# Inverse roots in seven dependent operations, and the first and last token groups gathered, added and stored in halves

## What is computed

```
def _layernorm(x, axis=-1, eps=1e-05):
    m = jnp.mean(x, axis=axis, keepdims=True)
    v = jnp.var(x, axis=axis, keepdims=True)
    return (x - m) / jnp.sqrt(v + eps)
...
x = x + jnp.tanh(g_xattn[0]) * _L0_xattn_ref(_layernorm(x, axis=-1), ctx_1024, ...)
x = x + jnp.tanh(g_ffn[0]) * _L0_ffn_ref(_layernorm(x, axis=-1), ...)
...
x = x + jnp.tanh(g_ffn[3]) * _L3_ffn_ref(_layernorm(x, axis=-1), ...)
```

```
sel = jnp.take_along_axis(expert_out, topk_idx[:, :, None], axis=1)
out = (sel * topk_scores.astype(flat.dtype)[:, :, None]).sum(axis=1)
out = out + jax.nn.silu(flat @ sgate_w.T) * (flat @ sup_w.T) @ sdown_w.T
```

## Time and profile before

| | us |
|---|---|
| median of 3 runs | 1399.87 |
| lowest and highest run | 1396.83, 1408.49 |
| the profiled execution | 1391.09 |
| its span, first to last instruction | 1389.3 |
| TensorE busy | 1218.6 |
| VectorE busy | 717.1 |
| mean granted TensorE clock | 0.916 |

### The profile page before, as it was taken

One profiled execution on the slowest core, in us unless ns is written; L12 is line 12 of the kernel. 1 busy time (PEld: TensorE's weight loads), 2 busy tenths in 40 slices (PEclk: granted clock), 3 DMA queues, 4 the chain that ended last, 5 costly groups with the idle time before them and its releaser, 6 DMA issues.

```text
span 1389.3 us, 19389 instructions
## 1 busy us (share of the span) xinstructions
PE 1218.6 (88%) x6360; PEld 765.9 (55%) x6361; DVE 717.1 (52%) x2061; ACT 448.6 (32%) x842; POOL 293.5 (21%) x347
## 2 busy tenths in 40 slices
PE   5999999999978899989988759999756799999993
PEld 3534434434443445444443649999655555888862
DVE  7263465376985466555752531111176752455556
ACT  3322122223353454454444103333233201333320
POOL 2111111040121111011000041111122564255660
PEclk9999999999988999999998669999976789999997
DMA  9999999110000000000100845555309322455538
GB/s 301 337 338 334 333 335 319 33 31 0 0 1 1 1 0 1 1 1 1 34 1 1 253 146 187 186 184 173 121 15 349 127 91 92 129 167 160 170 112 309
DMA packets 140424, 186.75 MB, mean 134 GB/s; under 512 B 8672, under 2 KB 124896, under 8 KB 140224
## 3 DMA queue, kind: packets, MB, share of 16 engines
q1 hardware_dynamic: 130800, 159.28, 37.0%
q0 software_dynamic: 9552, 26.52, 5.2%
HBM read 83.71 MB, written 102.06 MB: 134 GB/s over the span
## 4 chain that ended last, share of the span: by engine, by line
PE 74%; DVE 13%; ACT 4%; issue 3%; DMA 3%; POOL 2%; SPq 0%; POOLq 0%; DVEq 0%; ACTq 0%
PE psum L1979 14%; PE psum L1258 6%; PE psum L1269 6%; PE psum L1049 6%; PE psum L2191 5%; PE psum L1068 2%; PE psum L930 2%; PE psum L2248 2%; PE psum L2225 2%; PE psum L2272 2%; PE psum L1972 2%; PE psum L2007 2%; DVE arena L2810 2%; PE psum L2169 2%; PE psum L941 2%
## 5 line engine op out<-in xcount | busy, mean ns | idle before, releaser
L1979 PE MATMUL psum<-arena 128*128 128x512 f32 x432 | 205.1, 625 | 0.0
L2810 DVE TENSOR_REDUCE arena<-psum 128x4 f32<-128x616 f32 x128 | 101.6, 797 | 93.7 <-PE psum L2191 92.2
L1979 PEld LDWEIGHTS psum<-arena 128*128 128x128 f32 x432 | 82.9, 199 | 119.7 <-issue 118.9
L2191 PE MATMUL psum<-arena 32*128 32x308 f32 x512 | 103.5, 496 | 18.0 <-DVE arena L2810 16.8
L1176 POOL DMA_INDIRECT ys<-xnT,arena x96 | 92.4, 962 | 93.7 <-DVE xnT L1153 71.1
L2392 ACT ACTIVATE arena<-psum,arena 128x512 f32<-128x512 f32 x72 | 49.0, 685 | 174.3 <-PE psum L1979 164.6
L1870 POOL TENSOR_TENSOR x_tok<-x_tok,add_row 128x1024 f32<-128x1024 f32 x16 | 38.3, 2400 | 275.7 <-ACT xn L1735 275.6
L2483 ACT ACTIVATE arena<-psum 128x2048 f32<-128x2048 f32 x40 | 75.0, 1874 | 59.5 <-PE psum L2229 42.5
L1049 PE MATMUL psum<-arena,xn 128*128 x384 | 87.1, 380 | 2.3 <-ACT xn L1099 1.9
L1258 PEld LDWEIGHTS psum<-side,arena 128*128 128x128 f32 x736 | 87.4, 195 | 2.7 <-ACT side L1303 1.6
L1258 PE MATMUL psum<-side,arena 128*128 128x128 f32 x736 | 87.8, 278 | 1.0 <-ACT side L1303 1.0
(11 more groups left out here) (408 smaller groups left out, 2105.8 us busy)
## 6 DMA issues: line engine op xcount, KB each, us to landing
xs<-zeros SPq DMA_DIRECT2D x8, 8576.0 KB, 59.4
arena<-in_W SPq DMA_DIRECT2D x31, 1024.0 KB, 5.0
xn<-xs SPq DMA_DIRECT2D x64, 134.0 KB, 2.3
arena<-in_gate_up SPq DMA_DIRECT2D x4, 2048.0 KB, 15.7
arena<-ys SPq DMA_DIRECT2D x4, 2048.0 KB, 14.6
arena<-xs SPq DMA_DIRECT2D x32, 134.0 KB, 2.3
arena<-in_down SPq DMA_DIRECT2D x4, 1024.0 KB, 14.5
xs<-zeros SPq DMA_DIRECT2D x1, 2990.0 KB, 18.1
```

The source lines that it names most:

```text
L1979: ins = pe.matmul(bank[dict(hn=4, r=5, z=6, xn=7)[k]][:], lhs[:, cols], r, start=(start and n == 0), stop=(stop and n == len(w) - 1))
L2191: ins = pe.matmul(bank[most_bank(n, k) + i][:, 0:2 * M].rearrange("p (h m) -> p h m", h=2), qhT[rows, n % 3, c, t * P:(t + 1) * P], keys[r ...
L2810: dve.tensor_reduce(neg[:, n % 2, t, 2 * pair:2 * pair + 2, 2 * c:2 * c + 2], psum[:, most_bank(n, k):most_bank(n, k) + 2, 0:2 * M].rearra ...
```

## The change

The nine root steps become seven: one round of the old kind, with factors scaled by `CUBE_GAIN`, and one round of four operations of higher order (y*y; times v; plus a constant, times itself; plus a constant, times y). The start value stays. The list `endings` cuts the token tiles into six pieces: 0-1, 2-3, 4-7, 8-11, 12-13, 14-15. The gathers, the additions in `combine7_vector` and the stores go by these pieces, each with a semaphore of its own and its own count in `x_done`. On DVE the first three pieces (groups 0 and 1) stand before the shared expert's add for the last group, the other three behind it. The title given with the change also speaks of a moved context product; the diff has no edit of one.

```diff
-NEWTON = 3
+CUBE_GAIN = 0.375 ** 0.2
+RSQRT_STEPS = 7
...
+        first_gathered, last_gathered = sem("first_gathered"), sem("last_gathered")
+        endings = [(0, GT // 2, (first_gathered, 16))]
+        endings += [(g * GT + (GT // 2 if g == 0 else 0), (g + 1) * GT - (GT // 2 if g == G - 1 else 0), gathered_in[g].at(7, 16))
+                    for g in range(G)]
+        endings += [(T - GT // 2, T, (last_gathered, 16))]
...
-        xn_ready = Alternate(series("xn_ready_even", {s: G for s in (0, 2, 4, 6)}), series("xn_ready_odd", {s: G for s in (1, 3, 5, 7)}))
+        xn_ready = Alternate(series("xn_ready_even", {s: G for s in (0, 2, 4, 6)}), series("xn_ready_odd", {1: G, 3: G, 5: G, 7: G + 2}))
...
-            for g in range(G):
-                sp.dma_start(gathered7[:, g * GT:(g + 1) * GT],
-                             ys7[1 + g * GN * K4:1 + (g + 1) * GN * K4].rearrange("(t p k) d -> p t k d", p=P, k=K4)
-                             ).then_inc(gathered_in[g].sem, 16)
+            for t0, t1, landed in endings:
+                sp.dma_start(gathered7[:, t0:t1],
+                             ys7[1 + t0 * P * K4:1 + t1 * P * K4].rearrange("(t p k) d -> p t k d", p=P, k=K4)
+                             ).then_inc(landed[0], 16)
...
-        def combine7_vector(dve, ch, g):
-
-            dve.wait_ge(shared_added, 2 * (g + 1))
-            dve.wait_ge(*gathered_in[g].at(7, 16))
-            ch.settle()
-            xs = x_tok[:, g * GT:(g + 1) * GT]
+        def combine7_vector(dve, ch, n):
+
+            t0, t1, landed = endings[n]
+            dve.wait_ge(shared_added, 2 * (t0 // GT + 1))
+            dve.wait_ge(*landed)
+            ch.settle()
+            xs = x_tok[:, t0:t1]
             for k in range(K4):
-                ins = dve.tensor_tensor(xs, xs, gathered7[:, g * GT:(g + 1) * GT, k], ALU.add)
+                ins = dve.tensor_tensor(xs, xs, gathered7[:, t0:t1, k], ALU.add)
...
             combine7_vector(dve, ch, 0)
             combine7_vector(dve, ch, 1)
+            combine7_vector(dve, ch, 2)
             shared_add_vector(dve, G - 1)
-            combine7_vector(dve, ch, 2)
-            combine7_vector(dve, ch, 3)
+            for n in range(3, len(endings)):
+                combine7_vector(dve, ch, n)
...
-            for _ in range(NEWTON):
-                ch.settle(k)
-                ch.step(dve.tensor_tensor(t, y, y, ALU.mult))
-                k = ch.n
-                yield
-                ch.settle(k)
-                ch.step(dve.scalar_tensor_tensor(t, t, -0.5, v, ALU.mult, ALU.mult))
-                k = ch.n
-                yield
-                ch.settle(k)
-                ch.step(dve.scalar_tensor_tensor(y, t, 1.5, y, ALU.add, ALU.mult))
-                k = ch.n
-                yield
+            c = CUBE_GAIN
+            ch.settle(k)
+            ch.step(dve.tensor_tensor(t, y, y, ALU.mult))
...
+            ch.step(dve.scalar_tensor_tensor(t, t, -0.5 * c, v, ALU.mult, ALU.mult))
...
+            ch.step(dve.scalar_tensor_tensor(y, t, 1.5 * c, y, ALU.add, ALU.mult))
...
+            ch.step(dve.tensor_tensor(t, y, y, ALU.mult))
...
+            ch.step(dve.tensor_tensor(t, t, v, ALU.mult))
...
+            ch.step(dve.scalar_tensor_tensor(t, t, -1.25 / c ** 3, t, ALU.add, ALU.mult))
...
+            ch.step(dve.scalar_tensor_tensor(y, t, 1.875 / c, y, ALU.add, ALU.mult))
...
-        SLOT_STEPS = 2 + 3 * NEWTON + 2 * 2 + 2 * 1 + 2 * 1 + 8 * 3
+        SLOT_STEPS = 2 + RSQRT_STEPS + 2 * 2 + 2 * 1 + 2 * 1 + 8 * 3
...
-            for g in range(G):
-                sp.wait_ge(*x_done.at(last_stage, g + 1))
-                sp.dma_start(out.rearrange("(t p) d -> p t d", p=P)[:, g * GT:(g + 1) * GT],
-                             x_tok[:, g * GT:(g + 1) * GT]).then_inc(out_stored, 16)
-            sp.wait_ge(out_stored, G * 16)
+            for n, (t0, t1, _) in enumerate(endings):
+                sp.wait_ge(*x_done.at(7, n + 1))
+                sp.dma_start(out.rearrange("(t p) d -> p t d", p=P)[:, t0:t1], x_tok[:, t0:t1]).then_inc(out_stored, 16)
+            sp.wait_ge(out_stored, len(endings) * 16)
```

More of the change, by code:

```diff
@@ L1656, in rsqrt_newton @@
             k = ch.n
-            for _ in range(NEWTON):
-                ch.settle(k)
-                ch.step(dve.tensor_tensor(t, y, y, ALU.mult))
-                k = ch.n
-                yield
-                ch.settle(k)
-                ch.step(dve.scalar_tensor_tensor(t, t, -0.5, v, ALU.mult, ALU.mult))
-                k = ch.n
-                yield
-                ch.settle(k)
-                ch.step(dve.scalar_tensor_tensor(y, t, 1.5, y, ALU.add, ALU.mult))
-                k = ch.n
-                yield
+            c = CUBE_GAIN
+            ch.settle(k)
+            ch.step(dve.tensor_tensor(t, y, y, ALU.mult))
+            k = ch.n
+            yield
+            ch.settle(k)
+            ch.step(dve.scalar_tensor_tensor(t, t, -0.5 * c, v, ALU.mult, ALU.mult))
+            k = ch.n
+            yield
+            ch.settle(k)
+            ch.step(dve.scalar_tensor_tensor(y, t, 1.5 * c, y, ALU.add, ALU.mult))
+            k = ch.n
+            yield
+            ch.settle(k)
+            ch.step(dve.tensor_tensor(t, y, y, ALU.mult))
+            k = ch.n
+            yield
+            ch.settle(k)
+            ch.step(dve.tensor_tensor(t, t, v, ALU.mult))
+            k = ch.n
+            yield
+            ch.settle(k)
+            ch.step(dve.scalar_tensor_tensor(t, t, -1.25 / c ** 3, t, ALU.add, ALU.mult))
+            k = ch.n
+            yield
+            ch.settle(k)
+            ch.step(dve.scalar_tensor_tensor(y, t, 1.875 / c, y, ALU.add, ALU.mult))
+            k = ch.n
+            yield
             ch.settle(k)
```

## The result

The changed kernel took 1383.03 us in the median of 6 runs (1373.22 to 1386.56), the kernel before in runs on the same chip 1398.35 (6 runs, 1392.30 to 1408.49). The ratio is 0.9896, with a 95% interval from 0.9857 to 0.9935. Forecast were 1393.6 us, a range from 1385 to 1402, and a change within 1%.

What follows compares the result with a forecast made beforehand. The prediction took TensorE as three quarters of the chain, VectorE 13%. Root savings of 1.4 + 0 + 2.5 + 2.7 = 6.6 us and 0.3 lost in the ending gave -6.3: median 1399.87 to 1393.6 us, range 1385 to 1402.

Steps and rivals of the forecast that it cites:

- Start: First 20 us: two 308-wide steps, 1.02 us, plus two pairs of interleaved norm steps, 0.39, together 1.41 us less.
- Slot iterations: Three 128x16 roots lie hidden beside score products: 0 us gained, some 1.2 us at most without that cover.
- Attention stages: Stages with heads, 400 to 770 us: fewer norm steps on the chain, 2.5 us less, bounds 0 and 6.2.
- 58 x 2/9 x 0.196: Attention stages with heads: 58 root steps on the chain, two of nine go, 0.196 us each, 2.5 us saved.
- The upper bound of 6.2: Attention stages with heads: 16 norms saving 0.39 us each, 6.2 us at most.
- C: Rival: slower by TensorE's clock, 2.1 us per block falling to low; three eat the gain, five make 1404; chance 0.12.
- Rival D: Three blocks rising to high clock, 6.3 us, or attention stages 3.7 more: 1387 to 1390, both 1384; chance 0.11.
- a word against C: Argument that less waiting of TensorE should, if anything, leave the clock higher; no size given.
- The text's own sign of being wrong: Profile after: ending over 1 us shorter, slot iterations shorter, or stage lengths differing because the clock does.
- Last context attention: 1004 to 1105 us: seven norms fully on the chain, 0.39 us each, 2.7 us less, bounds 2 and 3.
- Ending: Output put together in six pieces: 0.73 us lost on VectorE, 0.4 gained by the smaller last store, 0.3 us slower.
- The wait for group 1: In the ending, VectorE waits some 1.8 us for group 1's gather; the shared add that could fill it stands behind.

Runs made afterwards that it cites:

- e12: Kernel before with seven root steps only in the three roots of the slot iterations, old ending: 1392.84 us, ratio 0.9993.
- e11: Changed kernel with a six-step root and the last group's shared add ahead of group 1's additions: 1390.09 us, ratio 0.9832.
- e3: Kernel before with only the ending in six pieces, the root in nine steps: 1393.61 us, ratio 1.0006.
- e6: Kernel before with seven root steps everywhere except the layer norms of stages 1 to 5, old ending: 1386.23 us, ratio 0.9944.
- e1: Kernel before, unchanged, run again against itself with a second profile: 1400.43 us, ratio 0.9999; profiled execution 1407.07 us.
- e2: Kernel before with only the root in seven steps, the ending as before: 1383.84 us, ratio 0.9907.
- e4: The changed kernel run once more, against the kernel before: 1385.89 us, ratio 0.9920.
- e5: Kernel before with seven root steps only in the layer norms of stages 1 to 5, old ending: 1388.78 us, ratio 0.9941.
- e8: Changed kernel with the last group's shared add moved ahead of group 1's additions; against the kernel before: 1383.30 us, ratio 0.9895.
- e9: Kernel before with the seven-step root made nine long by two dependent multiplications by 1.0, old ending: 1417.50 us, ratio 1.0024.
- e10: Kernel before with two rounds in the root, six dependent steps everywhere, old ending: 1390.04 us, ratio 0.9849.

## Why the prediction was wrong

**Start**: forecast -1.4 us, measured -1.3 by the means of six and five profiles. In the pair of profiles first compared it was -0.1, since the clock came back later (27.8 us, before 26.4): the eight 128x308 products behind the first transposes took 3.27 us after (from 25.71, L1917) and 2.24 before (from 26.70, L1893). Over more executions that evens out.

**Slot iterations**: forecast 0 with a bound of 1.2; e12 gave a ratio of 0.9993, and the lengths less half their time at the low clock show no gain. Right for these roots. The stretch itself varied from 299.8 to 316.5 us in profiles of kernels with the same nine steps in it, by the clock alone. It was 303.10 us in the three executions that came to it 67.6 to 67.7 us after the first product, all with the seven-step start, and 309.8 to 313.3 in the seven that came after 68.1 to 68.9; outside these it follows no order (306.41 after 67.23 in e11, 299.83 after 70.05 in e3). So whether the earlier start also makes the slot iterations shorter, by another phase of the clock, is open; e6's 8 us, where its path holds 4.6, would not need it, by its interval.

**Attention stages**: forecast -2.5 with a bound of 6.2, measured -8.3 (-7.8 without e1). This is the term that failed. Its step was "58 x 2/9 x 0.196": every root step on the chain as one unit of time, and the rest of the schedule left where it was. The runs showed two things in its place. The norms are dealt out in pieces behind reductions, so that two pieces fewer can move a norm's end past a reduction, which was worth 0.8 us where two steps are 0.4; at four places with equal time at the low clock the shorter path gave 3.6 us, more than the 2.5 for the whole stretch. And the places at which TensorE falls to half speed change: 0.39 us less of a pause was worth 3.3 at one, and a new fall cost 2.0 to 4.1 at another. In the sum the time at the low clock fell by 2.2 us only, which by the estimate above is 0.9 us, so the larger error is likely in the path; for some 4 of the 8.3 us it is open how they divide. The upper bound of 6.2 counted steps too, so it bounded nothing of this. The clock was in the text as rivals C and D, at 2.1 us for a block, but only as a thing of chance; that shorter pauses give fewer falls was written down as a word against C and wasn't given a price. The text's own sign of being wrong, stages whose lengths differ because the clock does, came: the slot iterations took 311.49 us (29.9 low) after 313.27 (33.3).

**Last context attention**: forecast -2.7 (2 to 3), measured -3.3, of which the steps are 2.7 (1.18 us for 1.57 in each of seven norms).

**Ending**: forecast +0.3 us, made of +0.7 on VectorE and -0.4 for the last store. Measured from the first gather's issue, by the means of nine profiles of the old ending and three of the new: VectorE's end +0.4 (29.19 and 29.56 us), from there to the end of the span -0.8 (3.35 and 2.57), together -0.4. The wait for group 1 (1.93 us) and the missed use of it were as forecast, and the last store was mis-sized. The estimate by the Trainium skill's figures (DMA: Bandwidth & Descriptors, the part on the fixed cost of a DMA) was 0.6 for it, and the rows here have 0.8. The whole is less than a time can tell, as e3 shows.

**From one execution to the median**: the sum was made against 1391.09 us and carried over as a difference. The profile of after came at 1382.49, only 2.3 us from the 1384.8 that the sum gave for it. But the profiled execution of before was quick in the attention stages (373.1 us, the other five 376.4 to 381.8), so that this pair of profiles alone shows 3.0 us there and hides the rest. That the two came so close was luck. Rival D held the outcome (1384 with both its parts at once), too cheaply: 0.11 for a gain that came again in e2, e4, e5 and e8.

## What to carry to other kernels

Before pricing a shorter dependent chain by its steps, look at what stands beside it. Where small work is dealt out in pieces between other operations, count the gaps it fills and not the pieces: two steps fewer gave 0.4 us for one norm and 0.8 for the next. Then list the pauses of TensorE that a granted clock near 0.5 follows: a block behind one of them costs some 3 us, and a shift by tenths of a microsecond can take such a fall away at one place and put it at another. So give the clock a range to both sides and no sum of blocks won. And look at more than one execution of the kernel before: here 26 runs of one program lay up to 19 us apart, more than the effect that was to be predicted.

## What the runs showed of the hardware

- The low clock falls in the same places of the program in many executions, but not in all: products 2730 to 2810 took 19.37 to 19.45 us with 6.8 us at the low clock in five of six profiles with nine steps in these norms, and 16.19 us with none in the sixth. A shorter chain moves the falls as well: products 2970 to 3130 had no low clock in six profiles with nine steps and 6.8 to 10.2 us in five with seven.
- VectorE's quantising operation of 128x1024 took 0.69 us alone and 2.71 us beside a GpSimd addition that reads and writes SBUF.
- The profiled executions beside six steps had the stages up to product 5500 as long as elsewhere, but the last one slower: products 5500 to 6359 took 198.51 us in e9, of which 17.1 at the low clock (187.13 in e10, 195.45 in e11), against 171.84 in the first profile. The weight loads of 1 MB (arena<-in_W) landed after 11.8 us in the median there, after 5.0 in the first profile. The runs of the kernel before beside them were 1.2% slower as well (1412.32 against 1395.49 us). The three kernels of that chip (e9, e10, e11) all had these landings at 11.8 to 12.0 us, and those on the other chips at 4.9 to 5.0; why is not shown. So a time is to be compared only with runs of before on its own chip.
